# The division of the softmax probabilities moved from GpSimd to VectorE, with their transposes behind it in two buffers

## The reference

```python
for i in range(DEPTH):                       # DEPTH = 6
    x = attn_layer(shift_tokens(x), Wqkv[i], q_scale[i], k_scale[i], Wo[i]) + x
    x = ffn_layer(shift_tokens(x), ln_g[i], ln_b[i], W1[i], b1[i], W2[i], b2[i]) + x

def attn_layer(x, Wqkv, qs, ksc, Wo):        # 16 heads of 64, windows of 32 tokens
    q, k, v = heads(x @ Wqkv)
    q = l2norm(q) * qs;  k = l2norm(k) * ksc
    q = q * cos * scale + rotate_half(q) * sin * scale
    k = k * cos / scale + rotate_half(k) * sin / scale
    sim = einsum('bhwie,bhwje->bhwij', q, look_back(k)) * 8.0   # 64 keys for each query
    attn = softmax(where(mask, -big, sim))
    return einsum('bhwij,bhwje->bhwie', attn, look_back(v)) @ Wo
```

## Time and profile before

| | us |
|---|---|
| median of 3 runs | 2908.08 |
| lowest, highest run | 2890.9, 2912.65 |
| the profiled execution | 2895.91 |
| its span in the trace | 2894.1 |

### The profile page before, as it was taken

How to read it: one execution, slowest core, us unless ns; L and a number is a source line. 1 busy time by engine, 2 the same in 40 slices (tenths; PEclk the granted TensorE clock), 3 DMA queues, 4 the chain that set the end, 5 groups by cost and what they waited for, 6 DMA issues and landing times.

```text
span 2894.1 us, 53763 instructions
## 1 busy us (share of the span) xinstructions
PE 2220.3 (77%) x21684; PEld 1186.8 (41%) x21780; DVE 1948.6 (67%) x2087; ACT 1536.6 (53%) x1859; POOL 1470.0 (51%) x1031
## 2 busy tenths in 40 slices
PE   4678758788888888888888888888888756788253
PEld 1111124455555455545555555545555311112253
DVE  2676457888778878787778887887877246763101
ACT  2255745665666666656656665666665223546100
POOL 5500047776676667666667766766766153000202
PEclk8698989999999999999999999999999766989686
DMA  5100000000010000000010001000000010000122
GB/s 154 50 21 26 1 1 16 1 2 16 1 25 2 16 1 10 16 16 1 1 25 1 16 2 25 2 16 1 9 2 1 0 60 32 23 23 16 41 76 65
DMA packets 55828, 59.08 MB, mean 20 GB/s; under 512 B 13142, under 2 KB 45012, under 8 KB 55508
## 3 DMA queue, kind: packets, MB, share of 16 engines
q1 hardware_dynamic: 53444, 50.77, 5.9%
q0 software_dynamic: 2128, 4.72, 0.7%
HBM read 44.07 MB, written 11.01 MB: 19 GB/s over the span
## 4 chain that ended last, share of the span: by engine, by line
PE 47%; issue 13%; ACT 13%; POOL 12%; DVE 11%; DMA 2%; SPq 1%; POOLq 0%; ACTq 0%; DVEq 0%
PE bank L855 7%; PE bank L929 6%; PE bank L919 5%; PE bank L731 5%; PE bank L702 4%; DVE big L1452 3%; PE bank L898 3%; ACT pxs L1301 2%; POOL big L576 2%; POOL big L593 2%; ACT L1323 2%; PE bank L958 2%; POOL big L577 2%; ACT big L1176 2%; PE bank L966 2%
## 5 line engine op out<-in xcount | busy, mean ns | idle before, releaser
L598 POOL TENSOR_TENSOR sc<-sc,small 128x1024 f32<-128x1024 f32 x96 | 263.4, 2744 | 467.3 <-DVE small L1594 467.3
L1452 DVE TENSOR_REDUCE big<-bank 128x1 f32<-128x512 f32 x512 | 328.6, 685 | 199.1 <-PE bank L702 194.8
L1292 ACT ACTIVATE sc<-sc 128x1024 f32<-128x1024 f32 x96 | 101.5, 1057 | 532.2 <-DVE sc L1584 532.2
L855 PE MATMUL bank<-wqk,xs 128*128 128x512 f32 x768 | 364.8, 617 | 13.4 <-ACT xs L1257 8.3
L929 PE MATMUL bank<-pxs,mw 128*128 128x256 f32 x1536 | 366.2, 382 | 0.0
L929 PEld LDWEIGHTS bank<-pxs,mw 128*128 128x128 f32 x1536 | 291.1, 192 | 100.9 <-issue 70.3
L1176 ACT ACTIVATE big<-bank 128x1024 f32<-128x1024 f32 x256 | 250.1, 1026 | 139.6 <-PE bank L716 136.8
L1558 DVE TENSOR_TENSOR big<-big,rotCl 128x2048 f32<-128x2048 f32 x96 | 222.4, 2317 | 79.2 <-POOL big L577 79.2
L702 PE MATMUL bank<-pxs 48*128 48x512 bf16 x512 | 186.1, 445 | 116.1 <-DVE big L1452 72.1
L1552 DVE TENSOR_REDUCE small<-big 128x32 f32<-128x2048 f32 x96 | 219.0, 2281 | 38.2 <-ACT big L1270 28.5
L1573 DVE TENSOR_TENSOR big<-big,small 128x1024 f32<-128x1024 f32 x192 | 241.0, 1256 | 1.1 <-POOL small L588 1.1
(11 more groups left out here) (237 smaller groups left out, 4035.4 us busy)
## 6 DMA issues: line engine op xcount, KB each, us to landing
wqk<-in_L_ffn_w SPq DMA_DIRECT2D x32, 256.0 KB, 3.1
wqk<-in_L_ffn_Wqkv SPq DMA_DIRECT2D x12, 512.0 KB, 4.3
pxs<-part_rows SPq DMA_DIRECT2D x64, 96.0 KB
pxs<-part_rows SPq DMA_DIRECT2D x64, 64.0 KB
wvt<-in_wv_layers_t SPq DMA_DIRECT2D x6, 512.0 KB, 5.1
wol<-in_L_ffn_Wo SPq DMA_DIRECT2D x6, 512.0 KB, 5.5
part_rows<-big SPq DMA_DIRECT2D x24, 128.0 KB
part_rows<-sc SPq DMA_DIRECT2D x24, 128.0 KB
```

The source lines that it names most:

```text
L598: pool.tensor_tensor(p3, p3, rden(i).unsqueeze(2).broadcast_to([P, LH, 64]), ALU.mult).then_inc(l_pn, 1)
L855: m = pe.matmul(bank[:, 2 - 2 * half + c, :], xs[:, b % 2, WIN + i * P:WIN + (i + 1) * P], wqk[:, (2 * half + c) * 512:(2 * half + c + 1) ...
L1452: dve.tensor_reduce(nm[:, qt, 2 * p + r:2 * p + r + 1], bank[:, 4 + r, :], AX.X, ALU.max, negate=True).then_inc(a_mx, 1)
```

## The change

POOL's slot loses `normalise`. DVE's slot gains it, behind `scaled(T + 1, half 1)`, and directly behind it `turn_probs(T)`, which stood in the next slot. The turned probabilities go into sc[:, 2, :] and sc[:, 3, :] in turn, `weigh` reads the one of its tile, and `turn_probs(T)` waits for the `weigh` of T-2 in place of T-1.

```diff
@@ POOL
-            def normalise(T, i):
-                pool.wait_ge(l_rd, T + 1)
-                p3 = probs(i).rearrange("p (h j) -> p h j", j=64)
-                pool.tensor_tensor(p3, p3, rden(i).unsqueeze(2).broadcast_to([P, LH, 64]), ALU.mult).then_inc(l_pn, 1)
-
             def slot(it, l, b, i, ahead):
...
                     add_keys(T + 1, (i + 1) % 2)
-                normalise(T, i)
                 if ahead >= 2:
...
@@ PE
             def weigh(T, i):
 
-                p4 = sc[:, 2, :].rearrange("p (h v t) -> p h v t", h=LH, v=2)
+                p4 = sc[:, 2 + i % 2, :].rearrange("p (h v t) -> p h v t", h=LH, v=2)
@@ DVE
+            def normalise(T, i):
+                dve.wait_ge(l_rd, T + 1)
+                p3 = probs(i).rearrange("p (h j) -> p h j", j=64)
+                dve.tensor_tensor(p3, p3, rden(i).unsqueeze(2).broadcast_to([P, LH, 64]), ALU.mult).then_inc(l_pn, 1)
+
             def turn_probs(T, i):
-                if not (isinstance(T, int) and T == 0):
-                    dve.wait_ge(l_px, 2 * T)
+                if not (isinstance(T, int) and T < 2):
+                    dve.wait_ge(l_px, 2 * T - 2)
                 dve.wait_ge(l_pn, T + 1)
                 settle(dve)
-                dve.transpose(sc[:, 2, :], probs(i)).then_inc(l_pt, 1)
+                dve.transpose(sc[:, 2 + i % 2, :], probs(i)).then_inc(l_pt, 1)
@@ DVE, slot
                     square_sums(T + 1, (i + 1) % 2)
-                if not (first and i == 0):
-                    turn_probs(T - 1, (i - 1) % 2)
                 if ahead >= 1:
                     turn_plain(T + 1, (i + 1) % TILES)
...
                 if ahead >= 1:
                     scaled(T + 1, (i + 1) % 2, 1)
+                normalise(T, i)
+                turn_probs(T, i)
                 if i == 1 and feeds:
...
@@ DVE, behind the slots
-            turn_probs(DEPTH * BATCH * TILES - 1, 1)
```

## The result

| | before | after |
|---|---|---|
| median, us | 2903.66 (4 runs) | 3053.89 (4 runs) |
| lowest, highest | 2890.9, 2912.65 | 3049.93, 3066.24 |
| the profiled execution | 2895.91 | 3066.24 |

The change made the kernel slower: 1.0528 times the time of before, with a 95% interval of 1.0475 to 1.0582. The forecast was 3056 us.

A forecast was written before the change was run, and what follows sets the result against it. DVE was taken to bound three slots of four, PE's scores the slot 0 to 1. 22 passes of 7.3 us (161), +10, −6 and −5 gave +160 on 2895.9: 3056 us, own range 3020 to 3085, wider range 2975 to 3105.

The forecast's parts named there:

- POOL slips in: At the k half's end POOL's L576 goes ahead of DVE's division; +2.4 us in three slots of four; chance 0.70.
- Slot 2 to 3: Between these row maxima, the division waits for L576 and `turn_plain` starts at 1234.7 instead of 1232.39: +2.3 us.
- Slot 3 to 0: Centring delays the k half, L576 gets in ahead of it, and L577 ahead of the division: +2.5 us.
- a loop body's end: Behind each of five loop bodies PE ends last and takes some 1.1 us of the slot's increase: −6 us.
- Slot 1 to 2: Division and transpose delay the first `hidden`; `turn_plain` starts at 1217.9 against 1215.41: +2.5 us.
- PE, 4.1 us late, is just hidden: In slot 1 to 2, PE, late by 3.7 us after some catching up, stays hidden against DVE's 2.1 + 2.5.
- PE becomes the bound: Rival: in slot 1 PE's delay decides, costing 4.1 instead of 2.5 us; 35 us more, 3091 us; chance 0.10.
- Slot 0 to 1: Collisions add some 3 us to DVE's row, under 5.43 us of idle time waiting for PE: 0.
- not slipping in: Rival: DVE keeps its place from k half to division; at most +0.7 us per pass, 2911 us; chance 0.10.
- not meeting: Rival: L576 comes up only when DVE is past the division; 25 us gained, 2871 or 2860 us; chance 0.05.

The follow-up runs named there:

- the hold to the k half: Changed kernel with POOL held ahead of `turn_swapped` only until DVE's k half has ended (wait for l_yk); 2882.41 us, 0.9937 times before.
- The hold to the end of the division: Changed kernel with POOL held ahead of `turn_swapped` until DVE's division has ended (wait for l_pn); 2891.03 us, 0.9966 times before.
- the first `hidden` ahead: Changed kernel with slot 1's first `hidden` product ahead of the division, the second behind the transpose; 2985.11 us, 1.0293 times before.

## Why the prediction was right

**The mechanism** is shown. One wait on POOL that changes only the moment it comes up takes the division from 3.33 to 1.21 us and the kernel from 3053.89 to 2882.41 us. The step "POOL slips in" was read from the pairs of 0.45 us instructions in `tables` (five of six pairs show it) and held for the 1.2 us division.

**The sum** was +160 us on a profiled execution of 2895.9. Against the medians the change measured 150 us, and in the layers of the two profiled executions 152.8: the forecast was 5 to 7% too large. That 3056 lies only 2 us from 3053.89 is luck: the profiled execution it starts from stood 8 us under the median of before, and the sum was 10 us too large. By slots:

*Slot 2 to 3*, forecast +2.3, measured +2.04 over all passes and 1.8 in a regular one (16.37 to 18.17). I had added each DVE instruction's full duration, but the next starts some 0.08 us ahead of the end of the last (1305.99 ahead of 1306.07 above), and L576 held the division for 2.19 us (1306.07 to 1308.26), not 2.35: several such steps are the 0.5 us. The mean is larger than the regular slot because in four passes PE's scores now end it, with DVE idle for 2.1 us (20.4 us).

*Slot 3 to 0*, forecast +2.5, measured +1.66. In a regular pass it was +2.0 (17.5 to 19.5), for the same reason. At a loop body's end DVE had waited 1.5 to 2.4 us for PE's scores before and waits no longer, so these four grew by 1.4 only; that I had counted, for five. In the five passes that also make the mixing weights DVE's centring (L303) waits for PE (1.3 to 1.9 us, before and after), the k half comes up when L576 is well on its way and takes 1.5 to 1.8 us instead of 2.75, so they grew by 0.9; that I had not counted.

*Slot 1 to 2*, forecast +2.5, measured +2.69, but not as I said. Where PE's clock stayed up it was +2.2 (18.07 to 20.30). "PE, 4.1 us late, is just hidden" holds for those slots, 3 of 21; in the other 18 PE worked at a lower clock afterwards and the slot took 21.1 to 23.1 us. In 13 of the 18 it grew by 3.6 us (18.1 to 21.7). In the other five, those with `tables`, it grew by 0.7 us only (22.0 to 22.7), and here I had left out a gain: the very collision of the earlier trace rows is gone. POOL's `add_keys` now comes up behind both L1611 (L1612 before), which take 0.85 us together instead of 2.95:

```profile
1381.90 0.85 DVE L1611 TENSOR_TENSOR rotSl<-rotS,qks 128x256 f32<-128x256 f32 x2
```

So the nearly right mean came of a term too large, a cost that I had left out and a gain that I had left out, about 10 us in all for the gain: luck. The rival that PE becomes the bound, to which I gave 0.10, was true in part: in 13 of the 21 slots DVE was idle for PE's scores at the end, for 0.1 to 1.0 us, and the second `hidden` waited for its product (2.25 us in the slot that begins at 850.91, where it was 1.31 in the one at 1193.05, with the clock up).

*Slot 0 to 1*, forecast 0, measured +0.36: hidden, as said. The idle time of DVE there fell from 5.43 to some 4.2 us, not to 2.5: the free L1547 (1.87 us in this slot before, 0.18 after) and the lost wait for L577 (1.16 us) gave back more of the slot than I counted.

**The durations** were given as 3.5 us for the division (3.33 as a mean, 3.37 as a median), 3.2 us for L576 in slots 1 and 2 (3.05), 0.2 us for L1547 (0.187), DVE busier by 275 us (2218.3 − 1948.6 = 269.7).

**The edits costed at nothing**: the second buffer is 0 by its own run. The move of the transpose was counted inside each slot's chain and not by itself; with the division on DVE it costs 33 us by the layers (37 to 44 by the medians).

**The rivals**: the hold to the k half comes near to "not slipping in", priced at 2911 us, 15 above the starting point; it measured 2882.41, 14 below its kernel before. The hold to the end of the division is "not meeting", priced at 2860 to 2871 us, 25 to 36 below; it measured 2891.03, 5 below. So both prices were wrong, and even their order. In both runs the slot from 1 to 2 with `tables` takes 19.97 us instead of 22.0, some 10 us that neither price had. For L1553 I had counted 46 us from its median; from its mean of 1.022 us it was 80 us in all, in the changed kernel too.

The GPSIMD Engine Reference of the Trainium skill (Key points) calls the DVE about twice as fast for elementwise work; the division took 1.21 us against POOL's 1.90, so here it was 1.6 times, and the whole kernel became slower all the same. The rule of the Trainium skill in SBUF — State Buffer (Who interferes with whom), that issue order decides who blocks, is the one that the runs bear out: in the changed kernel POOL's L576 was taken up ahead of the division (1305.21, 1305.99) and the division stood; held to the k half, the division was ahead (1224.76, 1225.10) and L576 stood.

## What to carry to other kernels

Work that is moved off GpSimd frees GpSimd to start its next instruction sooner, and where that next one and the moved one both want two SBUF operands they may meet: look at what each engine will have waiting at the end of the instruction ahead, not only at the length of what is moved. Such a meeting can be mended by one wait on the engine that has time (171 us here), or by putting an instruction with a PSUM operand where the other would stand. When a move delays a step that another engine waits for, put that step ahead of what was moved. And when a move shifts one engine against another, look also for the collisions of before that it takes away.

## What the runs showed of the hardware that I had not expected

*The wait also has a price in PE's clock.* Three slots from 1 to 2 of the kernel after, columns as in the windows above; the last but two is the granted clock:

```profile
1193.05:1213.35 20.30, 16.55 (x197) 10.06 (x198) 18.43 (x16) 9.51 (x11) 9.66 (x7) 1.00 0.01 2
1361.18:1383.72 22.54, 18.54 (x197) 11.53 (x198) 20.02 (x18) 9.52 (x11) 11.88 (x8) 0.92 0.15 48
1952.99:1975.41 22.42, 19.20 (x195) 12.18 (x195) 18.59 (x15) 9.51 (x11) 11.16 (x8) 0.83 0.01 1
```

In the second DVE also makes the layer's tables; the first and third hold the same work of DVE. In the first PE kept a granted clock of 1.00 and the slot took 20.30 us; in the third it had 0.83 and the slot took 22.42. PE stood idle for `hidden` in each (3.2 to 3.8 us over the 21 slots), and from there on its instructions may take nearly twice as long:

```profile
1373.03 1.47 PE L960 MATMUL bank<-xc,w 128*128 128x512 f32 x2 [3.74 <-DVE hT L1638]
...
1374.71 1.91 PE L860 MATMUL bank<-ident,big 128*128 128x128 f32 x8
```

The eight transposes L860 took 1.91 us here, behind 3.74 us of PE idle; in the first of the three slots, behind 3.75 us, they took 1.04 us. The clock's two levels are 1.2 and 2.4 GHz, and a mean of 0.83 says that PE was at the lower one for a part of the slot. Over the 21 slots after, 18 show a mean of 0.83 to 0.93, against 0.97 to 1.00 in all of before; with the first `hidden` ahead, where PE waits less than 0.5 us for it, it is 0.97 to 1.00 in all 21 again. Of the 16 slots without `tables`, the 13 at the lower mean took 21.7 us and the three spared 20.3: 1.4 us each. The other runs fit in. With the transpose back in its old place PE waited 1.9 to 2.4 us, and 15 of the 21 slots show 0.89 to 0.92; with POOL held it waited 0.9 to 1.6 us, and all show 0.96 to 1.00. Why 3 slots of 21 were spared with the same idle time stays open; no run was made for it.

*The two engines take turns in both directions.* In 94 of the 96 tiles a half of POOL's `turn_swapped` got in between DVE's k half and its division, with hardly a spread (each of these divisions took 3.35 to 3.40 us; the last two, with no `turn_swapped` ahead of them, took 1.21 and 1.23). And a waiting DVE instruction got in between POOL's two halves: in a regular pass the division in the slots from 1 to 2 and from 2 to 3, and the k half in the other two, where the division then waited for the second half.
